# A four-layer cross-attention block: how the second expert's share is formed, by weight differences or by masked inputs

## The reference

```python
vm = (tt[:, :-1] == 1) & (tt[:, 1:] == 1)        # last token of a sequence: never
x = rms_norm(hidden_states, ln_in_w)
mixed = jnp.where(vm, x @ v_qkv, x @ l_qkv)      # self-attention with rotary positions
attn_out = jnp.where(vm, ctx @ v_dense, ctx @ l_dense)
...                                              # cross-attention: one set of weights
mi = rms_norm(hidden_states, ln_post_attn_w)
v_out = silu(mi @ v_gate) * (mi @ v_up) @ v_down # 256 -> 688 -> 256
l_out = silu(mi @ l_gate) * (mi @ l_up) @ l_down
hidden_states = hidden_states + jnp.where(vm, v_out, l_out)
```

## Time and profile before

| | us |
|---|---|
| median of 3 runs | 2689.42 (2686.3 to 2690.03) |
| the profiled execution | 2684.68 |
| its span, first to last instruction | 2682.8 |
| TensorE matmul busy in it | 2560.8 (95%) |
| VectorE / ScalarE / GpSimd busy | 1534.7 / 1222.7 / 1155.9 |

### The profile page before, as it was taken

One profiled execution on the slowest core, in us unless ns is written; L12 is line 12 of the kernel. 1 busy time (PEld: TensorE's weight loads), 2 busy tenths in 40 slices (PEclk: granted clock), 3 DMA queues, 4 the chain that ended last, 5 costly groups with the idle time before them and its releaser, 6 DMA issues.

```text
span 2682.8 us, 54240 instructions
## 1 busy us (share of the span) xinstructions
PE 2560.8 (95%) x20342; PEld 1554.7 (58%) x20342; DVE 1534.7 (57%) x3448; ACT 1222.7 (46%) x4274; POOL 1155.9 (43%) x1242
## 2 busy tenths in 40 slices
PE   6999999999999999999999999999999999999998
PEld 3556556665565656566555565665656556566565
DVE  2537556766434646776644464677644456467763
ACT  2335444644333635464433362654544346265462
POOL 0025265665211527656410342765641034267564
PEclk9999999999999999999999999999999999999999
DMA  8010011112201011121220101112121000120211
GB/s 211 1 32 2 22 44 48 41 41 72 72 2 32 2 41 40 32 58 31 70 68 1 32 2 52 38 28 60 29 72 60 9 25 2 52 60 10 55 41 44
DMA packets 171100, 109.61 MB, mean 41 GB/s; under 512 B 31764, under 2 KB 168408, under 8 KB 170712
## 3 DMA queue, kind: packets, MB, share of 16 engines
q1 hardware_dynamic: 166384, 105.82, 14.2%
q10 hardware_dynamic: 4456, 0.29, 0.2%
HBM read 101.87 MB, written 4.19 MB: 40 GB/s over the span
## 4 chain that ended last, share of the span: by engine, by line
PE 82%; DVE 11%; POOL 2%; issue 2%; ACT 1%; ACTq 1%; DMA 0%; SPq 0%; DVEq 0%
PE bank L1358 10%; PE bank L1375 6%; PE bank L1081 6%; PE bank L995 5%; PE bank L1244 4%; PE bank L1251 4%; PE bank L1263 4%; PE bank L1272 4%; PE bank L1364 3%; PE bank L1116 2%; PE bank L1298 2%; PE bank L1098 2%; PE bank L1057 2%; PE bank L1224 2%; PE bank L1070 2%
## 5 line engine op out<-in xcount | busy, mean ns | idle before, releaser
L1861 POOL TENSOR_TENSOR Ebuf<-Ebuf,row_rcp 128x512 f32<-128x512 f32 (+1 forms) x328 | 345.8, 1060 | 797.4 <-DVE row_rcp L1684 796.3
L1463 ACT ACTIVATE Ebuf<-bank,minus_max 128x64 f32<-128x64 f32 x1312 | 392.4, 334 | 39.8 <-DVE minus_max L1668 39.5
L1668 DVE TENSOR_REDUCE minus_max<-bank 128x8 f32<-128x512 f32 (+1 forms) x328 | 219.8, 673 | 161.2 <-PE bank L1070 81.2
L1463 ACT ACTIVATION_READ_ACCUMULATOR Ebuf<-bank,minus_max 128x1 f32 x1312 | 297.4, 227 | 0.0
L1472 ACT ACTIVATE PT<-bank 128x512 f32<-128x512 f32 (+1 forms) x328 | 192.6, 601 | 152.5 <-PE bank L1081 151.0
L1081 PE MATMUL bank<-ident,Ebuf 128*128 128x128 f32 x1296 | 201.5, 283 | 9.9 <-POOL Ebuf L1861 9.4
L1081 PEld LDWEIGHTS bank<-ident,Ebuf 128*128 128x128 f32 x1296 | 146.4, 143 | 64.5 <-issue 39.2
L1358 PE MATMUL bank<-xs_a,w_ring 128*128 128x512 f32 (+1 forms) x384 | 172.2, 611 | 7.7 <-POOL w_ring L1909 7.3
L1358 PE MATMUL bank<-xs_b,w_ring 128*128 128x512 f32 (+1 forms) x384 | 169.1, 602 | 5.9 <-POOL w_ring L1909 3.9
L1456 ACT ACTIVATE Ebuf<-Ebuf 128x512 f32<-128x512 f32 x160 | 102.0, 638 | 101.6 <-DVE Ebuf L1673 99.5
L1908 POOL TENSOR_TENSOR w_ring<-w_ring 128x256 f32<-128x256 f32 x192 | 131.9, 708 | 0.0
(11 more groups left out here) (325 smaller groups left out, 5599.6 us busy)
## 6 DMA issues: line engine op xcount, KB each, us to landing
w_ring<-in_L_W SPq DMA_DIRECT2D x64, 256.0 KB, 3.0
w_ring<-in_L_l_gate SPq DMA_DIRECT2D x80, 128.0 KB, 2.2
w_ring<-in_L_l_up SPq DMA_DIRECT2D x80, 128.0 KB, 2.3
w_ring<-in_L_l_down SPq DMA_DIRECT2D x80, 128.0 KB, 2.2
w_ring<-in_L_v_gate SPq DMA_DIRECT2D x80, 128.0 KB, 2.4
w_ring<-in_L_v_up SPq DMA_DIRECT2D x80, 128.0 KB, 2.4
w_ring<-in_L_v_down SPq DMA_DIRECT2D x80, 128.0 KB, 2.5
arena_a<-in_x SPq DMA_DIRECT2D x4, 512.0 KB
```

The costliest lines, as they stand in the source:

```text
L1463: last = A(Ebuf[:, u % UNITS, cell], bank(token)[:, cell], ACT.Exp, bias=minus_max[:, u % UNITS, c:c + 1], accum_out=row_sum[:, u % UNITS, ...
L1668: V.reduce_max(minus_max[:, u % UNITS, 0:g], cells(bank(token)[:, 0:g * S]), AX_X, negate=True).then_inc(maxed, 1)
L1861: G_.tensor_tensor(v, v, row_rcp[:, n % 3, 0:g].unsqueeze(2).broadcast_to([P, g, S]), ALU.mult).then_inc(probs_ready, 1)
```

## The change

The difference weights go. The `v` weights are used as they are loaded, and the `l` side gets an input with the rare tokens masked out: l·(x·is_l) + v·(x·is_v). VectorE makes the masked inputs. The order of all steps is worked out anew by the same planner, with other costs for the changed steps. TensorE's own instructions (fillers apart) and the loads are the same in number and size.

```diff
 # planner
-        steps += [(max(0.0, 6.4 * j - 9.0), "weigh", n, j), (6.4 * j, "g", n, j), ...
+        steps += [(6.4 * j, "g", n, j), ...
-        own = chain(("PE", ...), ("DVE", {0: 1.5, 1: 2.45, 2: 2.45, 4: 0.95, 7: 0.95, 5: 1.15, 8: 1.15}.get(n, 1.75)))
+        own = chain(("PE", ...), ("DVE", {0: 1.5, 1: 2.45, 2: 2.45, 4: 0.95, 7: 0.95, 5: 2.0, 8: 2.0}.get(n, 3.45)))
-    if step == "weigh":
-        return [("POOL", 1.7, None)]
     if step == "u":
-        return chain(*(...), ("DVE", 1.0), ("POOL", 1.4))
+        return chain(*(...), ("DVE", 2.4), ("POOL", 1.4))
-        "silu": (("DVE", 0.9), ("POOL", 0.45)),
+        "silu": (("DVE", 0.9),),
 # TensorE
-                            pe.wait_ge(w_weighed, n - 1)
+                            pe.wait_ge(w_loaded[n], 16 * 9)
                         if step == "g":
-                            pe.wait_ge(*weighed[s].at(turn, FT * (n - 2) + j + 1))
+                            pe.wait_ge(*there)
 # step down
-                        pe.wait_ge(*h_ready[s].at(turn, FT * (n - 2) + j + 1))
+                        pe.wait_ge(*hl_ready[s].at(turn, FT * (n - 2) + j + 1))
 # VectorE, step masks
-                    V.memset(st.all[:, :], 1.0).then_inc(masks_ready[s].sem, 1)
+                    V.tensor_scalar(st.is_l[:, :], st.is_v[:, :], -1.0, 1.0, ALU.mult, ALU.add).then_inc(masks_ready[s].sem, 1)
 # VectorE, step spread (norms 3, 5, 6, 8 now write xv first)
+                    if n in (3, 6):
+                        for m in range(DT):
+                            dve.wait_ge(*normed[s].at(turn, STEP_AT[n] + m + 1))
+                            V.tensor_tensor(st.xn[:, m, :], st.xv[:, m, :], st.is_l[:, :], ALU.mult).then_inc(xn_ready[s].sem, 1)
+                    if n in (5, 8):
+                        dve.wait_ge(*normed[s].at(turn, STEP_AT[n] + 2 * h + 2))
+                        V.tensor_tensor(st.xn[:, :, at], st.xv[:, :, at], both(st.is_l[:, at]), ALU.mult).then_inc(xn_ready[s].sem, 1)
                     if n in LATE_AT:
-                        V.tensor_tensor(late(st.xv[:, :, at]), late(st.xn[:, :, at]), late(both(st.is_v[:, at])), ALU.mult).then_inc(xv_late[s].sem, 1)
+                        v = late(st.xv[:, :, at])
+                        V.tensor_tensor(v, v, late(both(st.is_v[:, at])), ALU.mult).then_inc(xv_late[s].sem, 1)
 # VectorE, step u
-                    V.scalar_tensor_tensor(out=st.hid_l[...], in0=v, scalar=0.5, in1=up, ...).then_inc(h_ready[s].sem, 1)
-                    dve.wait_ge(*sv_ready[s].at(turn, k + 1))
-                    V.scalar_tensor_tensor(out=hv, in0=hv, scalar=0.5, in1=by_batch(up)[:, :, LATE:S], ...).then_inc(hv_late[s].sem, 1)
+                    V.scalar_tensor_tensor(out=v, in0=v, scalar=0.5, in1=up, ...).then_inc(h_ready[s].sem, 1)
+                    dve.wait_ge(*h_ready[s].at(turn, k + 1))
+                    V.tensor_tensor(st.hid_l[...], v, st.is_l[0:rows, :], ALU.mult).then_inc(hl_ready[s].sem, 1)
+                    V.tensor_tensor(hid_v late columns, v late columns, st.is_v late columns, ALU.mult).then_inc(hv_late[s].sem, 1)
 # GpSimd: line 1870, step weigh and the silu part are taken out
-                            last.then_inc(w_weighed, 1)
-                if step == "weigh":
...
-                if step == "silu":
...
 # GpSimd, step u: reads silu_g in place of hid_l
```

More of the change, by code:

```diff
@@ L415, in room @@
         key = where[0] if where else None
[L416 to L420, removed]
         if step in FILL_STEPS and parts(step, where)[0][0] == "PE":
@@ L503, in schedule @@
             heads[step, s].pop()
[L504 to L507, removed]
             for j, (other, _, follow) in enumerate(pieces):
@@ L551, in schedule, with weight_chunks @@
             over[token] = max(end[token, other] for other, _, _ in pieces)
-ORDER, PAUSES, BEGIN, END, BANK, HELD, CHUNK_USES = schedule(global_order())
+def weight_chunks(order):
+    chunks = []
+    for step, s, turn, *where in order:
+        if step == "l1h" and where[0] % 2 == 0:
+            chunks.append((("f1", s, turn, where[0] // 2), ("w2", s, turn, where[0] + 1)))
+        if step == "g":
+            chunks.append((("ffn", s, turn, *where), ("down", s, turn, *where)))
+    return chunks
+ORDER, PAUSES, BEGIN, END, BANK, HELD = schedule(global_order())
 BEFORE_TABLE = set(ORDER["PE"][:ORDER["PE"].index(("table", 0, 0)) + 1])
-CHUNKS = {chunk: n for n, (chunk, _) in enumerate(CHUNK_USES)}
-CHUNK_ENDS = [ends for _, ends in CHUNK_USES]
+CHUNKS = {chunk: n for n, (chunk, _) in enumerate(weight_chunks(ORDER["PE"]))}
+CHUNK_ENDS = [ends for _, ends in weight_chunks(ORDER["PE"])]
 def transfers():
@@ L681, in xattn_kernel @@
         st.masks = sb(f"masks_{x}", [P, 2, T], BF16)
-        st.all, st.is_v = st.masks[:, 0, :], st.masks[:, 1, :]
+        st.is_l, st.is_v = st.masks[:, 0, :], st.masks[:, 1, :]
         media = sb(f"media_{x}", [P, PAIRS * S // 2])
@@ L811, in emptied @@
         if step in ("g", "u"):
-            return {"g": g_ready, "u": hv_late}[step][s].at(turn, FT * li + last + 1)
+            return {"g": g_ready, "u": h_ready}[step][s].at(turn, FT * li + last + 1)
         if step == "qk":
@@ L1343, in stages @@
                         rows = P if j < FT - 1 else FR
-                        ring, _ = chunk("ffn", s, turn, n, j)
+                        ring, there = chunk("ffn", s, turn, n, j)
                         w = ffn_weights(ring)[0][step]
@@ L1874, in _ @@
                     at = span(n, h)
[L1875 removed]
+                    pool.wait_ge(*xn_ready[s].at(turn, XN_AT[n] + (h + 1 if n in HALVED else 2)))
                     for m in range(DT):
[L1877 to L1878 removed]
+                        v = by_batch(st.xv[:, m, at])[:, :, 0:LATE]
+                        last = G_.tensor_tensor(v, v, by_batch(st.is_v[:, at])[:, :, 0:LATE], ALU.mult)
                     last.then_inc(xv_early[s].sem, 1)
@@ L1899, in _ @@
                         G_.tensor_tensor(*cross_blocks(st, p, r), ALU.mult).then_inc(kbd_built[s].sem, 1)
[L1900 to L1909, removed]
-                if step == "silu":
[L1911 to L1916, removed]
-                                     by_batch(st.is_v[0:rows, :])[:, :, LATE:S], ALU.mult).then_inc(sv_ready[s].sem, 1)
                 if step == "u":
```

65 lines of the change are left out of this document (25 added, 40 removed).

## The result

| | median us | ratio to the kernel before (95% interval) |
|---|---|---|
| before, same chip | 2689.73 | |
| changed | 2662.91 (2661.15 to 2667.34) | 0.9904 (0.9887 to 0.9921) |

The time is outside the forecast's range (2682 to 2748) and on the other side of no change. It is, to the microsecond, the price of rival A (2662), to which I had given a chance of 0.18. That the number is so close is luck: what A counted on did not happen, as the part on the prediction's steps shows.

What follows compares the result with a forecast made beforehand. TensorE bounds the kernel, busy 2560.8 us; only 231 us of waits and fillers can change. Terms 16 + 11 + 6 + 4 − 13.3 = +24 us on 2684.68, plus 4.7, gave 2713 us; 8-in-10 range 2682 to 2748.

Steps and rivals of the forecast that it cites:

- rival A: GpSimd's relief wins: shorter GpSimd queue and VectorE lines like 1807 less blocked, −18 us in the phases; 2662 us, chance 0.18.
- what TensorE gets back for certain: TensorE's 11.2 us of waits on GpSimd's differences and 2.10 us behind line 1870 go: −13.3 us.
- VectorE's gain: Work added to VectorE by products in chunks and norms, with blocking by GpSimd: between 115 and 247 us, taken as +180.
- What of it reaches TensorE: Delay to TensorE from VectorE's added work, in four terms: 16 + 11 + 6 + 4 us.
- Term 1: Longer VectorE queue in the twelve two-expert phases adds slack: +16 us, ends 0 and 43.
- The missing trend among the phases: Among a turn's three phases the busiest on VectorE has the least slack, so much slack comes from dependences.
- the slope to the quiet stretch: From quiet stretch (737 to 871 us) to phases, slack rose 0.3 points per VectorE point; that would give 43 us.
- Term 2: Start of qk, 16 times: first half of the norm's output ready 0.7 us later; +11 us, ends 0 and 23.
- Terms 3 and 4: First g waits for one product more, +6 us; last down of each feed-forward waits for the product, +4 us.
- work that the change leaves alone: TensorE's busy time without fillers, 2451.5 us, was taken as fixed; only slack could grow or shrink.
- that cover: Loads are issued four chunks ahead of use, so the new wait on the load itself is hidden: 0 us.

Runs made afterwards that it cites:

- e1: Kernel before, GpSimd's weight differences left out, TensorE waiting for the loads themselves, order, fillers and VectorE's work unchanged: 2649.55 us, ratio 0.9860.
- e2: Kernel before without weight differences, removed from the planner too, so newly planned, and without masked products: 2646.07 us, ratio 0.9846.
- e3: Changed kernel in its own order, without VectorE's products with is_l; the late product of a chunk stays: 2652.41 us, ratio 0.9870.
- e4: Changed kernel with the differences put back on GpSimd and into the planner, besides the masked products: 2707.75 us, ratio 1.0080.
- e5: Kernel before in its order, each chunk's three GpSimd subtractions replaced by fills of about equal time that read nothing, still waited for: 2660.45 us, ratio 0.9887.
- e6: Kernel before in its order, each chunk's subtractions done on a spare tile, TensorE waiting for the loads instead: 2677.11 us, ratio 0.9949.
- e12: Changed kernel's work, planned with the kernel before's prices for VectorE's part of u and of the norms: 2705.84 us, ratio 1.0049.
- e13: Kernel before, with the planner's price for a chunk's differences at 2.4 us for 1.7, nothing else changed: 2701.78 us, ratio 1.0052.

## Why the prediction was wrong, by its own steps

The prediction's sum runs over slack (waits and fillers) and takes TensorE's other work as fixed. Here are both in the profiles, us, with the mean granted clock. They are single executions, so small differences should not be read.

| | slack | other work | clock |
|---|---|---|---|
| before | 231.3 | 2451.5 | 0.993 |
| changed | 217.5 | 2441.8 | 0.997 |
| e1, no differences, order of before | 198.4 | 2448.6 | 0.992 |
| e2, neither, own plan | 189.4 | 2455.8 | 0.992 |
| e3, no products, order of changed | 209.8 | 2440.1 | 0.995 |
| e4, both, own plan | 258.1 | 2445.2 | 0.996 |
| e5, fills, order of before | 212.2 | 2449.9 | 0.994 |
| e6, idle differences, order of before | 221.9 | 2453.2 | 0.991 |
| e12, changed, old prices | 223.5 | 2473.3 | 0.989 |

**The step that failed: "what TensorE gets back for certain", −13.3 us.** I counted as GpSimd's cost only waits that the trace puts down to GpSimd. The differences' going was worth 36 us (e1, same order), 33 of them slack; with a plan of its own for each kernel it is 42 us of slack without products and 41 with them. The missing part is GpSimd's reads on VectorE's small norm instructions. It was in my own rows under another name: 25.3 us of waits for line 1731. I even used them against rival A ("TensorE's other waits are nearly all for VectorE"). I had applied the port to the large products that the change adds, and not to what was already there.

**VectorE's gain was right.** Forecast +180 us. Measured +144, net of the 35 us that e1 shows it was relieved of: 179. That relief was not in my sum. The block on the late product came in 92 of 96 chunks (0.72 us); the product with `is_l` mostly took its 0.69. GpSimd ended at 960.3 us, not near 900: its mask in `u`, which runs beside the late product, took 128.9 us (line 1894) in place of 91.2 (line 1924).

**What of it reaches TensorE: forecast +37, measured +9** (e3 to changed, same order) or +16 (e2 to changed, each with its own plan). In slack, which is what the sum was of, it is 8 us in the same order, but 28 with its own plan (27 from before to e4). So the size was not far off, and most of it comes with the order and not with the products themselves.

- Term 1, +16: slack in the phases went from 11.5, 8.5 and 11.7 us to 12.7, 8.3 and 11.0 (length less busy plus fillers of 8.18, 5.79 and 6.81). No growth over the kernel before, with VectorE at 78%. The missing trend among the phases, which I had quoted, was the better guide than the slope to the quiet stretch.
- Term 2, +11: the delay is there. From the norm's first write to `qk` took 1.52 us before; now:

```profile
1094.22 1.35 DVE L1733 SCALAR_TENSOR_TENSOR xs_a<-xT_a,gains,bank 128x512 f32<-128x512 f32 x2
1095.49 1.57 DVE L1743 TENSOR_TENSOR xs_a<-xs_a,masks_a 128x512 f32<-128x512 f32 x2
1096.67 1.88 PE L982 MATMUL bank<-xs_a,w_l_qkv 128*128 128x512 f32 x4
```

  2.45 us, +0.93. Slack in them is 1.55 us, against 0.56. Over all 16 such stretches it is 14.8 us against 5.3, so +9.6, as forecast. But e3, in the same order and without the product, has 15.4 there. It is the planner that put waits and fillers in this place, and the product itself adds nothing.
- Terms 3 and 4, +10: the waits ahead of the first `g` are 2.4 us (line 1750), against 2.1. The wait for the last `down` is 1.8 us, against 1.05, as forecast. Yet the end (last `g` to the last instruction) took 46.20 us against 47.60, and its slack is 7.4 against 9.3, with 1.25 us of fillers in place of 3.90.

**The clock, a second step that failed.** I took 2451.5 us as work that the change leaves alone. The same instructions took 2441.8, 9.7 us less. The profiled execution of before ran at 0.993, of the changed kernel at 0.997: the first has eleven short stretches at half clock (1.2 GHz) ahead of the last microseconds, the second five. So of the 23.5 us between the two spans, 13.8 are slack and 9.7 are this. It is not only these two executions: the changed kernel's four runs were at 0.994 to 0.997, and the kernel before, in its 37 runs beside the experiments, at 0.986 to 0.994. e1 gained its 36 us without it, at 0.990 to 0.994. Why the changed order keeps more of the clock is open. It has more fillers (118.5 us), and e12, with the fewest (87.8), has the lowest clock; but e13 has 127.2 and 0.993 in its profile, and no run changed the fillers alone.

**Rival A's number was luck.** A was right that GpSimd's relief wins. But it took −18 us from the phases, by lines like 1807 being less blocked. That line (now 1803) has medians of 1.34 and 1.64 us in the two streams, against 1.28 and 1.40 before, and the phases of the second turn lost no slack. The 2662 came from other parts: slack by the norms, added slack by the new plan, and the clock.

**Loads.** No wait for `w_ring` appeared: that cover held.

## What to carry to other kernels

A wait is put down to the engine that ended it, not to the one that made it late. Before an engine is written off as "not waited for", look for instructions of *other* engines that are longer than their minimum while it is at work, above all short dependent ones: 0.16 us became 0.65 here, three in a row, on the path. Here 154 us of work added to VectorE cost 9 us in a fixed order, and the same work in another order 1.5%, much of it at a lower clock: with a planned order, a change and its plan are two changes. And work that a change leaves alone can still take another time: compare TensorE's busy time without fillers, too.

## What the runs showed of the hardware

- The block doesn't spare small instructions. One of 128x2 or 128x4 (line 1719), 0.16 us of work, took up to 0.97 us. GpSimd's subtractions made the nine small lines 34.6 us longer; fills on GpSimd, which read nothing, only 5.3 (204.0 us in e5, 198.7 in e1).
- It isn't limited to two inputs: line 1714, a TENSOR_SCALAR with one SBUF input, took 0.79 us beside line 1924 at 1158.17 us, against a minimum of 0.17.
- One kernel's granted clock differs between its runs. Of 12 runs of the kernel before on one chip, the shortest had 0.994 (2682.64 us) and the longest 0.987 (2696.38 us): 14 us with nothing changed. Two profiled executions should be compared only after their clocks.
